# A four-layer graph network: the lists of the matrix build are loaded for two buckets at once, and each range's first product opens its PSUM banks

## The chip, the cores and the metric

The kernel runs on 1 core of one Trainium2 chip, as one program. The metric is the device time in microseconds (us). Its engines are TensorE (PE; its weight loads are listed apart as PEld), VectorE (DVE), ScalarE (ACT), GpSimd (POOL) and SyncE (SP). A q behind an engine's name (DVEq, PEldq) marks an instruction of its sequencer, which computes registers, waits and branches.

## The reference, cut to what matters

Four graph layers with a layernorm after each work on 6250 nodes of 128 features and 100000 edges:

```
edge_index = jnp.stack([src, dst])
x = _layernorm(x + _L0_gnn_ref(x, edge_index, ...))   # two hops over the edges, then two linear layers
x = _layernorm(x + _L1_gnn_ref(x, edge_index, ...))   # hypergraph: nodes = src, hyperedges = dst (2500 of them)
x = _layernorm(x + _L2_gnn_ref(x, edge_weight, ...))  # weighted sum over edges
x = _layernorm(x + _L3_gnn_ref(x, edge_index, ...))   # attention over edges
# the sums over edges that the layers share
agg = segment_sum(norm[:, None] * x[src], dst, num_segments=n)
```

The change is in one preparatory stage that several of these sums use: a matrix `edge_counts` with a row for each node (as source) and a column for each of the first 2560 nodes (as destination), that holds how many edges go from the one to the other.

## The kernel before, in words

Earlier stages sort the edges into 49 buckets by source (`src >> 7`, so 128 nodes a bucket) and write them as tiles of 128 edges, one edge a partition. In `m.meta` each tile has, for each partition, its destination and its source.

`bucket_lists` finds, for each bucket, where three ranges of destinations lie in its tiles. The ranges are `PARTS = ((0, 1), (1, 3), (3, 5))`, in PSUM banks of `KB` = 512 columns: one bank, two banks, two banks. For each bucket and range it stores three integers in the table `m.startI`: the first tile, the number of pairs of tiles, and how many pairs all earlier lists have. So a bucket has 9 integers of 4 bytes, at 36 bytes times its number.

`build_counts` builds the matrix, a bucket at a time, in the phase "build". Four engines run the same walk over the buckets, each in its own program: bucket 0, then a loop of 24 rounds that does an odd bucket and then an even one. Within a bucket all is ordered by semaphores:

- PE and DVE each first load the bucket's 9 integers into registers (`lists`, the load is at L1130). `bounded` (L1135) prepares one of them.
- DVE makes, for each tile, two one-hot matrices in bf16: of the source within the bucket (L1202, 128 by 128) and of the destination within the range (L1204, 128 by 512 or by 1024). There are two buffers, one for each tile of a pair. DVE may fill a buffer once PE has released it (`used`); PE may use it once DVE has announced it (`ready`).
- PE opens the range's banks with a product of zeros (L1170), so that all real products can accumulate, then for each tile multiplies the one-hots into one bank or two (L1177), and at the end closes each bank with a product of one column (L1180), which announces `summed`.
- ACT copies each finished bank to an SBUF row (L1156) and announces `emptied`, for which L1170 waits in the next bucket. SP stores the row of 1.28 MB when five banks are in it (L1141).

The pairs of tiles are a loop with a register as its bound, at L1172 on PE and L1197 on DVE. All engines meet at a barrier before and after the phase, so that its length is that of its slowest chain.

## Time and profile before

| what | value |
|---|---|
| median of 3 runs | 7867.82 us (7810.16 to 7903.07) |
| the profiled execution, its own time | 7873.77 us |
| its span, first to last instruction | 7872.0 us |
| mean granted TensorE clock over the span | 0.76 |
| phase "build", about | 1735 to 2581 us |
| buckets, ranges in the build | 49, 147 |

The span is 1.8 us shorter than the execution's own time. Rows with "idle before" tell how long the engine did nothing ahead of an instruction and what released it; "issue" there means that the profile shows nothing it waited for, which is where its sequencer was still busy with registers, loads or branches. A granted clock of 1.00 is TensorE at 2.4 GHz and 0.50 at 1.2 GHz.

### The profile page before, as it was taken

The numbers are of one execution on the slowest core, as the hardware profiler recorded it, in microseconds if no ns is written. First come the engines' busy times: TensorE is split into PE (matmuls) and PEld (weight loads), VectorE is DVE, ScalarE is ACT, GpSimd is POOL, SyncE is SP. The second block draws the span as 40 slices with busy tenths as digits, with TensorE's granted clock in tenths as the row PEclk, the third lists the DMA queues.
The fourth block names the chain that finished last, engine by engine and source line by source line (L and its number), as shares of the span: only waits on it lengthen the run. The fifth ranks groups of instructions, "written<-read, shape, count | busy, mean of one in ns | idle before, by whom it ended". The sixth has DMA issues, their size and how long they took to land. (4 is left out here: it accounts for less than half of the span.)

```text
span 7872.0 us, 98123 instructions
## 1 busy us (share of the span) xinstructions
PE 3812.2 (48%) x16163; PEld 2422.8 (31%) x16164; DVE 3389.4 (43%) x11703; ACT 1127.3 (14%) x3853; POOL 3603.0 (46%) x3613
## 2 busy tenths in 40 slices
PE   1600150016666775775945554333333356666665
PEld 0300030001111342443423332232322256665663
DVE  4946370026666444114021113333333555665666
ACT  0000000001111000002000001000000244444443
POOL 0045777710000684660056664666666155555550
PEclk9999999987777896887955555555555578888886
DMA  9411111261111563652711111111111233333332
GB/s 129 72 30 36 48 42 53 53 23 78 75 78 73 202 210 106 220 168 87 274 43 45 45 45 42 45 44 43 44 44 44 48 95 95 95 98 95 95 98 35
DMA packets 674873, 648.60 MB, mean 82 GB/s; under 512 B 495848, under 2 KB 564441, under 8 KB 655638
## 3 DMA queue, kind: packets, MB, share of 16 engines
q1 hardware_dynamic: 546182, 379.55, 18.1%
q0 software_dynamic: 128384, 266.34, 12.2%
q14 instruction: 151, 1.24, 0.1%
q10 hardware_dynamic: 144, 1.28, 0.0%
q8 instruction: 12, 0.20, 0.0%
HBM read 502.61 MB, written 144.27 MB: 82 GB/s over the span
## 5 line engine op out<-in xcount | busy, mean ns | idle before, releaser
L828 POOL DMA_INDIRECT bucketed_edges<-edge_rows,idx x784 | 817.6, 1043 | 784.0 <-issue 725.3
L483 POOL DMA_INDIRECT gathered<-node_table,idx x576 | 624.4, 1084 | 1130.7 <-ACT idx L471 958.4
L1337 POOL DMA_INDIRECT gathered<-node_table_xq,idx x832 | 796.3, 957 | 752.8 <-issue 223.7
L359 POOL DMA_INDIRECT gathered<-node_table,idx x816 | 772.7, 947 | 495.9 <-issue 249.8
L374 PE MATMUL ps<-onehots,gathered 128*128 128x128 f32 x1632 | 430.6, 443 | 846.7 <-DVE agg L402 609.0
L663 POOL DMA_INDIRECT gathered<-node_table,idx x588 | 556.1, 946 | 330.7 <-issue 171.7
L430 PE MATMUL ps<-gathered,junk 128*128 128x512 f32 x1182 | 622.4, 636 | 125.7 <-DMA gathered<-edge_counts 125.6
L678 PE MATMUL ps<-onehots,gathered 128*128 128x128 f32 x1176 | 467.7, 501 | 409.3 <-DMA gathered<-node_table,idx 394.9
L374 PEld LDWEIGHTS ps<-onehots,gathered 128*128 128x128 f32 x1632 | 365.1, 327 | 912.2 <-issue 834.3
L1177 PE MATMUL ps<-onehots 128*128 128x512 bf16 x1152 | 472.4, 487 | 187.0 <-DVE onehots L1204 183.9
L678 PEld LDWEIGHTS ps<-onehots,gathered 128*128 128x128 f32 x1176 | 294.6, 311 | 582.4 <-DMA gathered<-node_table,idx 559.4
L389 DVE TENSOR_SCALAR onehots<-iota,off_t,ew_t 128x128 f32<-128x128 f32 x832 | 258.2, 368 | 411.1 <-issue 376.1
L1426 PE MATMUL ps<-Wh,attend_slots 128*128 128x128 f32 x1664 | 405.9, 330 | 59.0 <-issue 56.0
L1427 PE MATMUL ps<-side_rows,attend_slots 128*128 x1664 | 386.7, 319 | 24.6 <-issue 24.6
L863 PE MATMUL ps<-gathered 128*128 128x49 bf16 x784 | 125.1, 222 | 544.6 <-DVE gathered L846 427.4
L499 PEld LDWEIGHTS ps<-onehots,gathered 128*128 128x128 f32 x1152 | 229.4, 217 | 504.4 <-issue 356.0
L402 DVE TENSOR_TENSOR agg<-agg,ps 128x128 f32 x816 | 233.5, 286 | 346.0 <-issue 289.1
L694 DVE TENSOR_TENSOR onehots<-ps,off_members 128x512 f32<-128x512 f32 x150 | 103.2, 689 | 648.0 <-DMA gathered<-node_table,idx 341.2
L534 DVE TENSOR_TENSOR onehots<-ps,off_t 128x512 f32<-128x512 f32 x156 | 107.0, 690 | 608.4 <-remote 237.6
L1202 DVE TENSOR_SCALAR onehots<-iota_b,side_rows,bF 128x128 bf16<-128x128 bf16 x722 | 227.2, 315 | 326.9 <-issue 204.7
L499 PE MATMUL ps<-onehots,gathered 128*128 128x128 f32 x1152 | 257.1, 316 | 208.0 <-DMA gathered<-node_table,idx 92.9
L1426 PEld LDWEIGHTS ps<-Wh,attend_slots 128*128 128x128 f32 x1664 | 311.2, 232 | 87.7 <-issue 85.1
(373 smaller groups left out, 6729.2 us busy)
## 6 DMA issues: line engine op xcount, KB each, us to landing
gathered<-edge_counts SPq DMA_DIRECT2D x99, 1280.0 KB
edge_counts<-gathered SPq DMA_DIRECT2D x49, 1280.0 KB
gathered<-node_table,idx POOLq DMA_INDIRECT x1980
bucketed_edges<-edge_rows SPq DMA_DIRECT2D x52, 544.0 KB, 12.5
edge_rows<-bucketed_edges SPq DMA_DIRECT2D x208, 128.0 KB
gathered<-edge_counts SPq DMA_DIRECT2D x48, 512.0 KB
side_rows<-edge_counts SPq DMA_DIRECT2D x48, 512.0 KB
edge_rows<-in_edge_attr_dram SPq DMA_DIRECT2D x108, 128.0 KB
```

The lines of the kernel that those rows point to most:

```text
L359: nc.gpsimd.indirect_dma_start(g[:, k, :], None, table, bass.IndirectOffsetOnAxis(m.idx[:, k:k + 1], 0)).then_inc(S["landed"][k], 16)
L374: last = nc.tensor.matmul(m.ps[:, q, e * P:(e + 1) * P], g[:, k, :], m.oh[:, k, :], start=True, stop=True)
L430: mm = nc.tensor.matmul(m.ps[:, k, :], m.junk[:, j, :], row_piece(m, j, k), start=first, stop=False)
L483: nc.gpsimd.indirect_dma_start(g[:, k, :], None, a.table, bass.IndirectOffsetOnAxis(m.idx[:, k:k + 1], 0)).then_inc(S["landed"][k], 16)
L499: last = nc.tensor.matmul(sums[q % NS], g[:, k, :], m.oh[:, k, :], start=e == 0, stop=e == G - 1)
L663: nc.gpsimd.indirect_dma_start(g[:, k, :], None, a.table, bass.IndirectOffsetOnAxis(m.idx[:, k:k + 1], 0)).then_inc(S["landed"][k], 16)
L678: last = nc.tensor.matmul(m.ps[:, q, 0:P], g[:, k, :], m.oh[:, k, :], start=e == 0, stop=e == G - 1)
L828: nc.gpsimd.indirect_dma_start(a.bucketed, bass.IndirectOffsetOnAxis(m.idx[:, k:k + 1], 0), m.erow[:, k, :], None).then_inc(S["scattered"] ...
L1177: last = T.matmul(m.ps[:, k, :], ohs[h], ohd[h][:, (k - k0) * KB:(k - k0 + 1) * KB], start=False, stop=False)
L1337: nc.gpsimd.indirect_dma_start(g[:, k, :], None, a.table2, bass.IndirectOffsetOnAxis(m.idx[:, k:k + 1], 0)).then_inc(S["landed"][s], 16)
L1426: T.matmul(out, m.eT[:, 2 * h + e // 2, :], m.Wh[:, e % 2, :], start=True, stop=False)
L1427: last = T.matmul(out, m.ohT[:, G * h + e, :], m.side[:, bass.ds(start[e], P)], start=False, stop=True)
```

## The change

The table of integers is laid out anew, still 9 integers a bucket: first tile and pairs of each range, then the three counts of earlier pairs. The walk over the buckets becomes `walk_lists`: in the loop each of PE and DVE loads the 18 integers of an odd bucket and the even one behind it with one instruction, at the start of the odd bucket. On PE the first pair of tiles of a range is written ahead of the loop, and the product of its first tile overwrites the banks (`start=True`); the product of zeros is gone, and the wait for `emptied` is one for the range instead of one for each bank. For that each list has at least two pairs: the lengths are raised to 3 tiles, which counts as two pairs.

```diff
--- before.py
+++ after.py
@@ -45,6 +45,7 @@
 KW = NK * KB
 PARTS = ((0, 1), (1, 3), (3, 5))
 NR = len(PARTS)
+ROWL = 3 * NR
 WB = KB * max(b - a for a, b in PARTS)
 SPLIT = (E - (P - 1) * NT) // U
 DUMP = BT * P
@@ -1043,8 +1044,7 @@
     inb, rev, fwd, f = (m.gather[0:NB, k * BT:(k + 1) * BT] for k in range(4))
     one, two = m.gather[:, 4 * BT:5 * BT], m.gather[:, 5 * BT:6 * BT]
     first, past = m.lists[PB, 0:NR + 1], m.lists[PB, 6:7 + NR]
-    rowF = m.gather[0:1, 6 * BT:6 * BT + 3 * NB * NR]
-    three = rowF.rearrange("p (b k c) -> p b k c", k=NR, c=3)
+    rows = m.gather[0:1, 6 * BT:6 * BT + ROWL * NB].rearrange("p (b c) -> p b c", c=ROWL)
     pairs, ends = (m.gather[0:1, 7 * BT + j * NB * NR:7 * BT + (j + 1) * NB * NR] for j in range(2))
     halves = lambda t: t.rearrange("p (h t) -> p h t", h=2)
     with phase(nc, "lists", "dve cmp marked counted taken listed rows") as (S, block):
@@ -1075,18 +1075,21 @@
             step(V.tensor_scalar(first, first, -1.0, float(BT), ALU.mult, ALU.add))
             step(V.tensor_scalar(first, first, float(BT - 1), None, ALU.min))
             step(V.tensor_tensor(past, past, first, ALU.subtract))
-            V.tensor_scalar(past, past, 1.0, None, ALU.max).then_inc(S["listed"], 1)
+            step(V.tensor_scalar(past[:, 0:NR], past[:, 0:NR], 3.0, None, ALU.max))
+            V.tensor_scalar(past[:, NR:NR + 1], past[:, NR:NR + 1], 1.0, None, ALU.max).then_inc(S["listed"], 1)
             v.wait_ge(S["rows"], 2 * NR)
+            table = m.startI[0:1, 0:ROWL * NB].rearrange("p (b c) -> p b c", c=ROWL)
+            by_bucket = lambda t: t.rearrange("p (b k) -> p b k", k=NR)
             for q in range(NR):
-                step(V.tensor_copy(three[:, :, q, 0], m.ps[0:1, 5, q * NB:(q + 1) * NB]))
-                step(V.tensor_scalar(three[:, :, q, 1], m.ps[0:1, 5, (NR + q) * NB:(NR + q + 1) * NB], 1.0, None, ALU.add))
-            step(V.tensor_copy(m.startI[0:1, 0:3 * NB * NR], rowF))
-            step(V.tensor_scalar(m.startI[0:1, 0:3 * NB * NR].rearrange("p (i c) -> p i c", c=3)[:, :, 1],
-                                 m.startI[0:1, 0:3 * NB * NR].rearrange("p (i c) -> p i c", c=3)[:, :, 1], 1, None, ALU.arith_shift_right))
-            step(V.tensor_copy(pairs, m.startI[0:1, 0:3 * NB * NR].rearrange("p (i c) -> p i c", c=3)[:, :, 1]))
+                step(V.tensor_copy(rows[:, :, 2 * q], m.ps[0:1, 5, q * NB:(q + 1) * NB]))
+                step(V.tensor_scalar(rows[:, :, 2 * q + 1], m.ps[0:1, 5, (NR + q) * NB:(NR + q + 1) * NB], 1.0, None, ALU.add))
+            step(V.tensor_copy(table[:, :, 0:2 * NR], rows[:, :, 0:2 * NR]))
+            for q in range(NR):
+                step(V.tensor_scalar(table[:, :, 2 * q + 1], table[:, :, 2 * q + 1], 1, None, ALU.arith_shift_right))
+                step(V.tensor_copy(by_bucket(pairs)[:, :, q], table[:, :, 2 * q + 1]))
             step(V.tensor_tensor_scan(ends, m.ones[0:1, 0:1].to_broadcast([1, NB * NR]), pairs, 0.0, ALU.mult, ALU.add))
             step(V.tensor_tensor(ends, ends, pairs, ALU.subtract))
-            step(V.tensor_copy(m.startI[0:1, 0:3 * NB * NR].rearrange("p (i c) -> p i c", c=3)[:, :, 2], ends))
+            step(V.tensor_copy(table[:, :, 2 * NR:], by_bucket(ends)))
 
         @block.tensor
         def _(pe):
@@ -1125,14 +1128,23 @@
                 body(eng.snap(i * 2 + 1), 1, i)
                 body(eng.snap(i * 2 + 2), 0, i + 1)
 
-        def lists(eng, engine, b):
-
-            got = nc.values_load_multi_w_load_instructions(m.startI[0:1, bass.ds(b * (3 * NR), 3 * NR)], engines=[engine])[1]
-            return [got[3 * k:3 * k + 3] for k in range(NR)]
-
-        def bounded(eng, before):
-
-            return eng.snap(nc.s_assert_within(before, 0, NK * (BT + NB)))
+        def walk_lists(eng, engine, body):
+
+            def load(b, n):
+                got = nc.values_load_multi_w_load_instructions(m.startI[0:1, bass.ds(b * ROWL, n * ROWL)], engines=[engine])[1]
+                return [got[ROWL * k:ROWL * (k + 1)] for k in range(n)]
+            body(0, load(0, 1)[0])
+            with eng.Fori(0, (NB - 1) // 2) as i:
+                b = eng.snap(i * 2 + 1)
+                odd, even = load(b, 2)
+                body(b, odd)
+                body(eng.snap(i * 2 + 2), even)
+
+        def parts(eng, row):
+
+            bounded = lambda x: eng.snap(nc.s_assert_within(x, 0, NK * (BT + NB)))
+            for k, (k0, k1) in enumerate(PARTS):
+                yield k0, k1, row[2 * k], row[2 * k + 1], bounded(row[2 * NR + k])
 
         @block.sync
         def _(sp):
@@ -1162,23 +1174,22 @@
             pe.sem_inc(S["used"], 2)
             pe.sem_inc(S["emptied"], NK)
 
-            def body(b, e, u):
-                at = lists(pe, mybir.EngineType.PE, b)
-                for r, (k0, k1) in enumerate(PARTS):
-                    for k in range(k0, k1):
-                        pe.wait_ge(S["emptied"], b * NK + k + 1)
-                        T.matmul(m.ps[:, k, :], m.zerob[:, :], zeros, start=True, stop=False)
-                    n, before = at[r][1], bounded(pe, at[r][2])
-                    with pe.Fori(0, n) as j:
-                        c = pe.snap((before + j) * 2)
+            def body(b, row):
+                for k0, k1, lo, n, before in parts(pe, row):
+                    def pair(c, first):
                         for h in range(2):
                             pe.wait_ge(S["ready"], c + (h + 1))
                             for k in range(k0, k1):
-                                last = T.matmul(m.ps[:, k, :], ohs[h], ohd[h][:, (k - k0) * KB:(k - k0 + 1) * KB], start=False, stop=False)
+                                last = T.matmul(m.ps[:, k, :], ohs[h], ohd[h][:, (k - k0) * KB:(k - k0 + 1) * KB],
+                                                start=first and h == 0, stop=False)
                             last.then_inc(S["used"], 1)
+                    pe.wait_ge(S["emptied"], b * NK + k1)
+                    pair(pe.snap(before * 2), True)
+                    with pe.Fori(1, n) as j:
+                        pair(pe.snap((before + j) * 2), False)
                     for k in range(k0, k1):
                         T.matmul(m.ps[:, k, 0:1], m.zerob[:, :], m.zerob[:, 0:1], start=False, stop=True).then_inc(S["summed"], 1)
-            walk(pe, body)
+            walk_lists(pe, mybir.EngineType.PE, body)
 
         @block.vector
         def _(v):
@@ -1189,14 +1200,12 @@
             v.wait_ge(S["iota"], 1)
             step(V.tensor_copy(iotaK, iotaI))
 
-            def body(b, e, u):
-                at = lists(v, mybir.EngineType.DVE, b)
-                for r, (k0, k1) in enumerate(PARTS):
+            def body(b, row):
+                for k0, k1, lo, n, before in parts(v, row):
                     w = (k1 - k0) * KB
-                    lo, n, before = at[r][0], at[r][1], bounded(v, at[r][2])
                     with v.Fori(0, n) as j:
                         c = v.snap((before + j) * 2)
-                        t = v.snap(nc.s_assert_within(lo + j * 2, 0, BT, skip_runtime_bounds_check_because="a list ends at the last tile"))
+                        t = v.snap(nc.s_assert_within(lo + j * 2, 0, BT + 2, skip_runtime_bounds_check_because="a list ends at the last tile"))
                         for h in range(2):
                             v.wait_ge(S["used"], c + (h + 1))
                             V.tensor_scalar(ohs[h], m.iotab[:, :], m.meta[:, bass.ds(t + h, 1), 2], m.bF[:, bass.ds(b, 1)],
@@ -1204,7 +1213,7 @@
                             V.tensor_scalar(ohd[h][:, 0:w], iotaK[:, 0:w], m.meta[:, bass.ds(t + h, 1), 1], -float(k0 * KB),
                                             ALU.subtract, ALU.is_equal).then_inc(S["ready"], 1)
 
-            walk(v, body)
+            walk_lists(v, mybir.EngineType.DVE, body)
 
 
 def member_lists(nc, m):
```

PE, the loop of the walk, the start of the odd bucket's second range (destinations 512 to 1535, two banks), before. L1169 computes the wait's value, L1135 prepares the count of earlier pairs:

```order
L1180 MATMUL ps<-zero_b 128x1
L1169 ISA
L1170 MATMUL ps<-zero_b 128x512
L1169 ISA
L1170 MATMUL ps<-zero_b 128x512
L1135 ISA x2
L1172 UNCONDITIONAL_BRANCH
L1172 ISA
L1177 MATMUL ps<-onehots 128x512 x2
```

and the same place in the changed kernel:

```order
L1191 MATMUL ps<-zero_b 128x1
L1145 ISA x2
L1186 ISA
L1181 ISA
L1183 MATMUL ps<-onehots 128x512 x2
L1181 ISA
L1183 MATMUL ps<-onehots 128x512 x2
L1188 UNCONDITIONAL_BRANCH
L1188 ISA
L1183 MATMUL ps<-onehots 128x512 x2
```

The two products of zeros are gone, the products of the range's first two tiles stand ahead of the loop's branch, and only one instruction computes a wait on `emptied`.

DVE, the same loop, from the end of the odd bucket's last range to the first one-hot of the even bucket, before:

```order
L1204 TENSOR_SCALAR onehots<-junk,side_rows 128x1024
L1197 REGISTER_ALU
L1197 COMPARE_AND_BRANCH
L1130 ISA
L1130 TENSOR_LOAD start_i
L1135 ISA x2
L1197 UNCONDITIONAL_BRANCH
L1197 ISA
L1202 ISA x2
L1202 TENSOR_SCALAR onehots<-iota_b,side_rows,bF 128x128
```

and in the changed kernel:

```order
L1213 TENSOR_SCALAR onehots<-junk,side_rows 128x1024
L1206 REGISTER_ALU
L1206 COMPARE_AND_BRANCH
L1145 ISA x2
L1206 UNCONDITIONAL_BRANCH
L1206 ISA
L1211 ISA x2
L1211 TENSOR_SCALAR onehots<-iota_b,side_rows,bF 128x128
```

The load between the odd bucket and the even one is gone. The one at the start of the loop's round is still one instruction; it fills 18 registers where it filled 9.

## Rows read from the trace of the kernel before

**Rows 1.** Windows: the matrix build as one stretch (columns as its first line says)
```profile
core 0: us, PE busy (x) PEld busy (x) DVE busy (x) ACT busy (x) POOL busy (x), PEclk, DMA share, GB/s
...
1735.00:2580.00 845.00, 557.25 (x1642) 126.38 (x1642) 515.82 (x1446) 132.91 (x243) 0.67 (x1) 0.75 0.18 74
```

**Rows 2.** Lines by form, 1733 to 2585 us: busy us, mean ns | idle before, releasers
```profile
L1177 PE MATMUL ps<-onehots 128*128 128x512 bf16 x1152 | 472.4, 487 | 187.0 <-DVE onehots L1204 183.9
L1202 DVE TENSOR_SCALAR onehots<-iota_b,side_rows,bF 128x128 bf16<-128x128 bf16 x722 | 227.2, 315 | 326.9 <-issue 204.7 <-PE ps L1177 93.2
L1204 DVE TENSOR_SCALAR onehots<-junk,side_rows 128x1024 bf16<-128x1024 f16 x430 | 209.1, 486 | 0.6
...
L1170 PE MATMUL ps<-zero_b 128*128 128x512 bf16 x245 | 101.4, 488 | 105.7 <-issue 77.3 <-ACT gathered L1156 28.3
```

**Rows 3.** Source view of L1130, the list loads: all 49, then single ones
```profile
L1130 DVEq TENSOR_LOAD <-start_i x49: 862/2075/2099, 1736.5 to 2565.4; - x49
...
L1130 DVEq TENSOR_LOAD <-start_i x1: 864/864/864, 2009.1 to 2009.1; - x1
...
L1130 DVEq TENSOR_LOAD <-start_i x1: 2082/2082/2082, 2025.1 to 2025.1; - x1
...
L1130 PEldq TENSOR_LOAD <-start_i x1: 2427/2427/2427, 2025.7 to 2025.7; - x1
...
L1130 DVEq TENSOR_LOAD <-start_i x1: 2074/2074/2074, 2043.3 to 2043.3; - x1
```

**Rows 4.** Source views of other loads of the table: one value, four, sixteen
```profile
L646 DVEq TENSOR_LOAD <-start_i x50: 298/304/318, 3968.5 to 4808.4; - x50
...
L103 DVEq TENSOR_LOAD <-start_i x208: 340/344/357, 6342.7 to 7741.5; - x104
...
L103 DVEq TENSOR_LOAD <-start_i x8: 1098/1100/1111, 5391.8 to 5555.5; - x8
```

**Rows 5.** Timeline of DVE where a bucket's first range begins (start us, us)
```profile
2010.95 0.32 DVE L1202 TENSOR_SCALAR onehots<-iota_b,side_rows,bF 128x128 bf16<-128x128 bf16 x1 [1.71 <-issue]
...
2013.02 0.32 DVE L1202 TENSOR_SCALAR onehots<-iota_b,side_rows,bF 128x128 bf16<-128x128 bf16 x1 [0.65 <-PE ps L1177]
...
2028.08 0.31 DVE L1202 TENSOR_SCALAR onehots<-iota_b,side_rows,bF 128x128 bf16<-128x128 bf16 x1 [3.18 <-issue]
...
2029.90 0.32 DVE L1202 TENSOR_SCALAR onehots<-iota_b,side_rows,bF 128x128 bf16<-128x128 bf16 x1 [0.41 <-issue]
...
2046.35 0.31 DVE L1202 TENSOR_SCALAR onehots<-iota_b,side_rows,bF 128x128 bf16<-128x128 bf16 x1 [2.90 <-issue]
```

**Rows 6.** Timeline of PE about two range changes of one bucket
```profile
2017.01 1.02 PE L1170 MATMUL ps<-zero_b 128*128 128x512 bf16 x2
2017.94 1.83 PE L1177 MATMUL ps<-onehots 128*128 128x512 bf16 x4
...
2021.52 0.59 PE L1170 MATMUL ps<-zero_b 128*128 128x512 bf16 x2
2022.29 0.60 PE L1177 MATMUL ps<-onehots 128*128 128x512 bf16 x2 [0.18 <-DVE onehots L1204]
```

**Rows 7.** Timeline of DVE in the two-bank ranges of that bucket
```profile
2017.15 0.31 DVE L1202 TENSOR_SCALAR onehots<-iota_b,side_rows,bF 128x128 bf16<-128x128 bf16 x1 [0.67 <-PE ps L1177]
...
2019.36 0.32 DVE L1202 TENSOR_SCALAR onehots<-iota_b,side_rows,bF 128x128 bf16<-128x128 bf16 x1 [0.67 <-PE ps L1177]
...
2021.50 0.32 DVE L1202 TENSOR_SCALAR onehots<-iota_b,side_rows,bF 128x128 bf16<-128x128 bf16 x1 [0.54 <-issue]
...
2023.31 0.32 DVE L1202 TENSOR_SCALAR onehots<-iota_b,side_rows,bF 128x128 bf16<-128x128 bf16 x1 [0.27 <-issue]
```

**Rows 8.** Windows of that bucket, split where the granted clock changes
```profile
2012.80:2019.60 6.80, 4.91 (x12) 1.02 (x11) 4.31 (x13) 0.59 (x1) 0.00 (x0) 0.50 0.35 145
2019.60:2029.80 10.20, 5.33 (x22) 1.41 (x21) 5.62 (x16) 2.15 (x4) 0.00 (x0) 1.00 0.21 89
```

**Rows 9.** Groups by line, 1728 to 1735 us, the end of the list stage
```profile
L1084 DVE TENSOR_SCALAR start_i<-start_i 1x147 int32<-1x147 int32 x1 | 0.3, 252 | 0.0
```

## The prediction

> **What bounds the kernel now.** The change touches the end of the list stage and the phase "build"; nothing else. I read the windows first, to size the phase: 845 us of the span, with neither PE (557 us) nor DVE (516 us) busy all the time, the clock 0.75 on average and the DMA engines at 18% [rows 1]. So two engines take turns there, and the next view is the groups by line and form. DVE makes 722 pairs of one-hots, its idle time of 327 us stands before L1202 and most of it is "issue", that is, its own sequencer [rows 2]. PE's 245 products of zeros are 101 us busy [rows 2]. The reader is to ask of each whether it lies on the chain DVE to PE to DVE that paces the phase. The source view of L1130 and the timeline show where a bucket begins: DVE stands for 1.71, 3.18 or 2.90 us [rows 5] while the sequencer loads nine integers in 0.86, 2.08 or 2.07 us [rows 3]. Both engines load at about the same time, and neither has work for the other.
>
> **The load, which is the largest term.** The three single loads are of buckets 16, 17 and 18. The same instruction serves 16 and 18, so it is the address that makes 0.86 or 2.07 us. Through all 49 loads on DVE the pattern holds: the 13 buckets with a number divisible by four take 0.86 to 0.87 us (the very first 1.10), the other 36 take 2.07 to 2.10. A bucket's list starts at 36 bytes times its number, which is a multiple of 16 just for those 13. Other loads of the same table agree: one value 0.304 us, four values from a multiple of 16 bytes 0.344, sixteen 1.100 [rows 4]. From an aligned start the cost goes by groups of four: 0.344 + 3 x 0.25 = 1.10 for sixteen, and 0.344 + 2 x 0.26 = 0.86 for nine. From any other start it goes by single values: 0.304 + 8 x 0.2214 = 2.075 for nine.
>
> The new double load always starts at an odd bucket, never at a multiple of 16 bytes, and has 18 values: 0.304 + 17 x 0.2214 = 4.07 us against 2.08, so +1.99 us. Odd buckets in the loop are 24: **+47.8 us**. Bounds: if 18 values from there went by fours after all, five groups cost 0.344 + 4 x 0.25 = 1.34, -0.74 each or -18 us; above, PE's dearest load was 2.43 us [rows 3], by which 18 cost 0.304 + 17 x 0.266 = 4.82, with PE some 0.15 us late once DVE's two buffers are full, +4 us more. I take the price by single values, because nine odd-started values have it in 24 of 24 loads.
>
> The Trainium skill, "Runtime: NRT & Kernel Launch", section "Instruction fetch mechanics", puts such a load at about 200 ns a register even in bulk. This trace has 230 for nine unaligned values, and 96 and 69 for nine and sixteen aligned ones. By the page's rule 24 loads of 18 values cost what 48 of nine do, the two loads together would be near zero in place of +5.7, and the total +21.
>
> **The load that goes.** Even buckets in the loop are 24; 12 of them (16 and the like) begin with 1.71 us of idle DVE, 12 (18 and the like) with 2.90 [rows 5]. What is late next is what every change of range costs with no load: 0.54 at the high clock, where the last range ends, and 0.67 at the low one [rows 7]. At 0.55: 12 x (1.71 - 0.55) + 12 x (2.90 - 0.55) = **-42.1 us**. The two loads together: **+5.7 us**. ACT, which copies the banks out, and the stores behind it hold slack: 133 us of 845 busy and 18% of the DMA engines [rows 1], so nobody there waits for the shorter change of bucket.
>
> **The products of zeros.** They are 101 us of PE and I take them at nothing, by the timeline of PE. At the change from one bank to two, at the low clock, two of them run from 2017.01 to 2018.03 in the records, and the first real product starts at 2017.94 [rows 6], right behind the one-hot that DVE began at 2017.15 (0.31 + 0.49 us of work) [rows 7]. At the next change they run from 2021.52 and end at 2022.11, and PE waits 0.18 us more for DVE [rows 6]. At a bucket's start PE opens its bank while DVE makes its first one-hot. Bounds: 0, and -0.1 us for each of 98 inner changes, -10 us. The closing products of one column stay. Moving two first products ahead of PE's loop leaves their number: 1152. Had any list only one pair, the floor of two would add work; the one-hots, counted list by list in the timeline, give 2 or 3 pairs in all 147 lists (the third range has 2 in each of 49), so it adds none.
>
> **The clock.** The build swings between the two levels in every bucket. In the bucket of the rows TensorE is at 0.50 (1.2 GHz) from 2012.8 to 2019.6 and at 1.00 (2.4 GHz) to 2029.8 [rows 8]. It rose while six 512-column products stood nearly end to end (two of zeros, four real, 2017.01 to 2019.77) and fell after the load's gap and the thin one-bank work. The level is worth time only in the two-bank ranges: a pair of tiles takes 2019.36 - 2017.15 = 2.21 us at the low one, where DVE waits for PE, and 2023.31 - 2021.50 = 1.81 at the high one, where DVE paces [rows 7], 0.40 a pair. Without the products of zeros TensorE has a gap of 0.8 us just ahead of that rise. I expect it later in some buckets: if half of them do the two pairs of the last range at the low level, 49 x 0.5 x 2 x 0.40 = **+20 us**. Bounds: 0, and, if the clock stays low through all five banks' work, some 2.3 pairs a bucket, 49 x 2.3 x 0.40 = +45 us.
>
> **The rest.** The list stage gets one more step of the kind of L1084 and four more short ones, 0.25 us each [rows 9]: +1.2 us. The code also shifts, and that has a price which no row assigns beforehand: a pair in the one-bank range takes 2013.02 - 2010.95 = 2.07 us in the even bucket's copy of the loop and 1.82 in the odd one's [rows 5], with the same instructions. There are 48 such pitches in each copy, so +12 or -12 us; I take 0.
>
> **The sum.** 5.7 + 0 + 20 + 1.2 = +27 us on the profiled execution's 7873.8 us, 7901. That execution lies 6 us above the median of the runs, so I predict 7867.8 + 27 = 7895 us. The phase would grow from 846 to about 873 us.
>
> **The rivals.** (a) *The wide load is cheap.* If 18 values go by fours, the loads give -18 - 42 = -60 us, with the clock's +20 and the list stage -39: 7829. For it: aligned loads do so. Against it: 36 of 36 unaligned ones did not. (b) *The products of zeros held the clock up.* This is the slower side. Their place is the start of the two-bank ranges. If without them the clock rises in no bucket before the load's gap, the sum is 5.7 + 45 + 1.2 = +52, with the code's shift up to +64: 7920 to 7932. All other terms together are between +7 and, with the inner changes' whole 10 us gained, -3; so it decides the sign once about one bucket in ten keeps the low clock (0.1 x 45 = 4.5 us). It can't reach 1% by itself, which would be 79 us. For it: the rise follows dense work of which a third were zeros. Against it: the real products alone are still four in each 2.21 us. [...] (c) *The clock does not care.* The zeros were fewer than a fifth of PE's columns (245 of 1397 products), the rises stay where they are, and the sum is +7, or -3 with the inner changes: 7865 to 7875.
>
> **How the numbers follow.** Chances: forecast 0.45, (a) 0.12, (b) 0.18, (c) 0.25. A measurement of this kernel tells about 1% from no change: its three runs span 93 us, 1.2%. Even (a) is -0.5% and (b) +0.8%, so the chance that it is the same within 1% is 0.91; 0.04 for faster, if the loads and the layout both go well and the runs scatter low, and 0.05 for slower. The range must hold (a) nearly whole and (b) with its scatter: 7829 at the low end, 7932 at the high end, and some 10 us of scatter of a median of runs: 7825 to 7942.
>
> **What would show it.** The source view of the list load should have 24 loads of about 4.1 us and one of 1.1 on DVE; DVE's idle at an odd bucket's start about 5.1 us, and at an even one's 0.5 to 0.7. L1170 gone, 1152 products left. The mean clock of the build below 0.75, and more two-bank pairs at 2.21. I am wrong if the load of 18 takes under 3 us, or if two-bank pairs keep their 1.81 in the last range of nearly all buckets; and wrong in kind if a stage other than the build moves by more than 20 us.

## The result, and the profile after

The changed kernel takes 7921.56 us, the median of 15 runs (7895.68 to 7982.26), against 7856.02 for the kernel before in 15 runs of the same series. The ratio is 1.0089, with a 95% interval of 1.0067 to 1.0111: slower by 0.9%, some 70 us. The forecast was +27 us and 7895, with a range of 7825 to 7942. The time lies in the range, but the step is two and a half times as large as forecast.

The profiled execution took 7982.26 us (span 7980.5), the longest of the 15. Its first one-hot of the build starts at 1781.6 us, that of the kernel before at 1738.5: 43 us came in ahead of the build, where the program is the same but for 1 us of list steps. Over the profiled kernels of this study, which ahead of that point differ only in a few short steps (one with a phase of loads ahead of it is left out), the first one-hot lies between 1732 and 1806 us. So whole times of single executions are not compared below; the stretch from the first one-hot of the build to the last is. The windows view of that stretch, changed kernel (columns as in [rows 1]):

```profile
1781.60:2688.90 907.30, 517.53 (x1394) 112.61 (x1395) 514.50 (x1444) 132.83 (x243) 0.00 (x0) 0.67 0.17 69
```

The same stretch of the kernel before, a few us shorter than that of [rows 1]:

```profile
1738.40:2579.40 841.00, 556.07 (x1638) 125.99 (x1639) 514.41 (x1444) 132.91 (x243) 0.00 (x0) 0.75 0.18 75
```

It grew by 66 us at an unchanged busy time of DVE (514.5 and 514.4 us). The groups by line of the changed kernel, for [rows 2]:

```profile
L1183 PE MATMUL ps<-onehots 128*128 128x512 bf16 x1152 | 515.2, 531 | 398.9 <-DVE onehots L1213 385.6 <-ACT gathered L1168 12.5
L1211 DVE TENSOR_SCALAR onehots<-iota_b,side_rows,bF 128x128 bf16<-128x128 bf16 x722 | 227.2, 315 | 393.4 <-issue 254.4 <-PE ps L1183 109.3
```

DVE's idle time ahead of its one-hots is 393 us in place of 327, most of the growth under "issue"; each real product is 531 ns in the mean in place of 487, because more of them run at the low clock (the windows say 0.67 in place of 0.75). The products of zeros are gone. The source view of the list load, for [rows 3]:

```profile
L1134 PEldq TENSOR_LOAD <-start_i x25: 1048/6390/6457, 1778.2 to 2653.6; - x25
L1134 DVEq TENSOR_LOAD <-start_i x25: 1104/6269/6286, 1779.7 to 2653.0; - x25
```

Here is the term that was mis-sized: the 24 loads of 18 values take 6.13 to 6.29 us on DVE, where 4.07 was forecast. The timeline of DVE where a bucket begins, for [rows 5], first an odd bucket and then the even one behind it:

```profile
2060.30 0.32 DVE L1211 TENSOR_SCALAR onehots<-iota_b,side_rows,bF 128x128 bf16<-128x128 bf16 x1 [7.23 <-issue]
...
2076.75 0.31 DVE L1211 TENSOR_SCALAR onehots<-iota_b,side_rows,bF 128x128 bf16<-128x128 bf16 x1 [0.65 <-issue]
```

7.23 us idle in place of 3.18, and 0.65 in place of 1.71 or 2.90. And the two-bank pairs, for [rows 7], in the last range of the bucket before that:

```profile
2049.03 0.31 DVE L1211 TENSOR_SCALAR onehots<-iota_b,side_rows,bF 128x128 bf16<-128x128 bf16 x1 [0.54 <-PE ps L1183]
...
2051.24 0.32 DVE L1211 TENSOR_SCALAR onehots<-iota_b,side_rows,bF 128x128 bf16<-128x128 bf16 x1 [0.46 <-PE ps L1183]
```

That pair took 2.21 us in a range where it had taken 1.81. The stretch by its parts, from the starts of the one-hots and the idle times in the timeline:

| part | before, us | after, us | difference x count | us |
|---|---|---|---|---|
| DVE idle at the start of an odd bucket, mean | 3.17 | 7.34 | +4.17 x 24 | +100.2 |
| at the start of an even bucket, mean | 2.32 | 0.66 | -1.66 x 24 | -39.7 |
| one-bank pair in the even bucket, start to start | 2.06 | 1.81 | -0.25 x 47 | -11.6 |
| change from one bank to two, last start to first start | 2.07 | 2.08 | 0.00 x 49 | +0.1 |
| two-bank pairs: 13 us between their starts, 4 in the last one of each bucket | | | | +17.3 |
| sum | 841.0 | 907.3 | | +66.3 |

In the last range, the pair that can be timed (49 of them, one a bucket) took the high clock's 1.66 to 1.81 us in 42 buckets before and in 20 after. The change from one bank to two, where the products of zeros used to stand, takes as long without them.

### The profile page after: what moved, and what is told of

It is laid out like the page before. It is cut to its first block and busy times, and to the rows that moved or that the text cites. A ratio compares the mean times of both kernels' runs of the same rounds, so it can differ in the third digit from the quotient of the medians.

```text
span 7980.5 us, 97152 instructions
## 1 busy us (share of the span) xinstructions
PE 3777.5 (47%) x15918; PEld 2414.8 (30%) x15919; DVE 3393.4 (43%) x11708; ACT 1127.0 (14%) x3853; POOL 3576.9 (45%) x3613
## 5 line engine op out<-in xcount | busy, mean ns | idle before, releaser
L829 POOL DMA_INDIRECT bucketed_edges<-edge_rows,idx x784 | 798.2, 1018 | 845.5 <-issue 760.2
L375 PE MATMUL ps<-onehots,gathered 128*128 128x128 f32 x1632 | 430.6, 443 | 854.6 <-DVE agg L403 608.2
L1183 PE MATMUL ps<-onehots 128*128 128x512 bf16 x1152 | 515.2, 531 | 398.9 <-DVE onehots L1213 385.6
L679 PE MATMUL ps<-onehots,gathered 128*128 128x128 f32 x1176 | 467.7, 501 | 409.4 <-DMA gathered<-node_table,idx 398.1
L500 PE MATMUL ps<-onehots,gathered 128*128 128x128 f32 x1152 | 258.6, 317 | 206.4 <-DMA gathered<-node_table,idx 90.1
L1447 PE MATMUL ps<-onehots,gathered 128*128 128x128 f32 x1664 | 275.7, 316 | 128.7 <-DVE onehots L1482 88.4
```

The source lines that it names most:

```text
L375: last = nc.tensor.matmul(m.ps[:, q, e * P:(e + 1) * P], g[:, k, :], m.oh[:, k, :], start=True, stop=True)
L500: last = nc.tensor.matmul(sums[q % NS], g[:, k, :], m.oh[:, k, :], start=e == 0, stop=e == G - 1)
L679: last = nc.tensor.matmul(m.ps[:, q, 0:P], g[:, k, :], m.oh[:, k, :], start=e == 0, stop=e == G - 1)
L829: nc.gpsimd.indirect_dma_start(a.bucketed, bass.IndirectOffsetOnAxis(m.idx[:, k:k + 1], 0), m.erow[:, k, :], None).then_inc(S["scattered"] ...
L1183: last = T.matmul(m.ps[:, k, :], ohs[h], ohd[h][:, (k - k0) * KB:(k - k0 + 1) * KB], start=first and h == 0, stop=False)
```

## The experiments

The 18-value load was first measured by itself.

**Loads alone.** The kernel before, with a phase ahead of the build in which only DVE loads (the values are used as indices of a small copy, whose output nobody reads):

```diff
+            with v.Fori(0, 8) as i:
+                use(nc.values_load_multi_w_load_instructions(m.startI[0:1, bass.ds(i + 448, 1)], engines=[mybir.EngineType.DVE], ...)[1])
...
+                use(nc.values_load_multi_w_load_instructions(m.startI[0:1, bass.ds(i + 448, 20)], engines=[mybir.EngineType.DVE], ...)[1])
```

> The kernel before, with an extra phase of loads alone ahead of the build: VectorE loads 1, 2, 4, 5, 8, 9, 10, 12, 13, 16, 17, 18 and 20 values from each of 8 start places in a row (0 to 28 bytes past a multiple of 64), nothing else running. The phase computes nothing that is used. Theory A (the price is in the instruction: number of values and start place): 18 values from an unaligned start take 6.27 us here too, although PE is silent, and the steps show where the price leaves 0.22 us a value. Theory B (two engines in each other's way: PE and DVE load at once in the build): 18 values alone take 0.304 + 17 x 0.22 = 4.07 us, 20 take 4.5. Both: from multiples of 16 bytes the price goes by fours, 9 values 0.86, 16 values 1.10.

Source views of five of the lines, for 4, 9, 16, 18 and 20 values; each line ran from eight start places, two of which are multiples of 16 bytes. The three numbers are minimum, median and maximum in ns:

```profile
L1127 DVEq TENSOR_LOAD <-start_i x8: 352/958/965, 1759.2 to 2232.5; - x8
...
L1130 DVEq TENSOR_LOAD <-start_i x8: 849/2064/2067, 1765.8 to 2241.5; - x8
...
L1134 DVEq TENSOR_LOAD <-start_i x8: 1105/3603/3608, 1782.4 to 2264.3; - x8
...
L1136 DVEq TENSOR_LOAD <-start_i x8: 1579/4044/4049, 1794.5 to 2281.3; - x8
...
L1137 DVEq TENSOR_LOAD <-start_i x8: 1362/4484/4490, 1801.1 to 2290.3; - x8
```

The minimum is that of the two aligned starts, median and maximum those of the other six. From an unaligned start the price is 0.22 us a value up to twenty; 18 take 4.04 us, as the prediction had it. From an aligned start it goes by fours at 0.25 us each, and each value left over costs about as much as a group of four (18 values 1.58 us, 20 values 1.36). So theory A fell: the price of 6.27 us is not in the instruction. Something in the build adds 2.2 us.

**The double load undone.** The changed kernel, with one line for each bucket:

```diff
-                odd, even = load(b, 2)
-                body(b, odd)
-                body(eng.snap(i * 2 + 2), even)
+                body(b, load(b, 1)[0])
+                c = eng.snap(i * 2 + 2)
+                body(c, load(c, 1)[0])
```

> The changed kernel, but each bucket loads its own 9 values at its start, as before; the overwriting first product stays. From the first one-hot to the last the build took 840.9 us before and 907.2 after. Theory 'the wide load does the harm': 907.2 - 24 x (7.33 + 0.66) + 24 x 3.17 + 12 x 1.71 + 12 x 2.92 = 847 us, ratio to before about 1.001. Rival 'the overwriting product or the peeled pair does the harm': the build stays over 880 us and the ratio over 1.005.

```profile
1737.50:2587.10 849.60, 534.45 (x1394) 114.31 (x1394) 514.07 (x1444) 132.85 (x243) 0.00 (x0) 0.66 0.18 74
```

The ratio to before is 0.9979 (0.9950 to 1.0007), so the loss in the whole time is gone. Of the 66 us in the build 58 are, and those were the double load's. The build is still 9 us longer than the 841 of the kernel before, though it no longer has the dear one-bank pair (-12): the two-bank pairs cost 20 us more, at a clock of 0.66 in this row.

**The zeros put back.** The changed kernel with the product of zeros in place of the overwriting first one:

```diff
-                                                start=first and h == 0, stop=False)
+                                                start=False, stop=False)
...
-                    pe.wait_ge(S["emptied"], b * NK + k1)
-                    pair(pe.snap(before * 2), True)
-                    with pe.Fori(1, n) as j:
+                    for k in range(k0, k1):
+                        pe.wait_ge(S["emptied"], b * NK + k + 1)
+                        T.matmul(m.ps[:, k, :], m.zerob[:, :], zeros, start=True, stop=False)
+                    with pe.Fori(0, n) as j:
```

> The changed kernel, but with the products of zeros back (and no peeled pair on PE); the double load stays. Theory 'the clock was lost with the zeros': about 18 us come back against the changed kernel, the build takes 889 us, pairs in the third range are at 1.81 us again in at least 40 of 49 buckets, ratio to before 1.006. Rival 'the long gap behind the 18-value load lets the clock fall': the pairs at 2.21 us stay and the build takes 905 to 910 us.

```profile
1732.10:2628.10 896.00, 550.62 (x1638) 139.96 (x1638) 513.95 (x1444) 132.87 (x243) 0.00 (x0) 0.75 0.17 70
```

The ratio to before is 1.0077 (1.0043 to 1.0112). The clock is back at 0.75 with the long loads still there, and the pair in the last range is at 1.66 to 1.81 us in 44 of 49 buckets: the long gap is not what kept the clock low. The edit also puts the peeled pair back into its loop, and no run has the one without the other. But the peeled pair moved none of the real work: the change from one bank to two takes 2.07 or 2.08 us, and the pair behind it at the low clock 2.21, in the kernel before and in the changed one alike. What is left as the difference on PE is the zeros.

Only 11 us came back in place of 18. In this kernel the first two-bank pair at the low clock takes up to 2.36 us, in the kernel before 2.21. The timeline of PE and DVE at such a place:

```profile
2028.63 0.21 PE L1192 MATMUL ps<-zero_b 128*128 128x1 bf16 x1
2028.85 0.32 DVE L1212 TENSOR_SCALAR onehots<-iota_b,side_rows,bF 128x128 bf16<-128x128 bf16 x1 [0.68 <-PE ps L1183]
...
2028.93 1.03 PE L1188 MATMUL ps<-zero_b 128*128 128x512 bf16 x2
...
2029.76 1.91 PE L1183 MATMUL ps<-onehots 128*128 128x512 bf16 x4
```

The products of zeros start 0.30 us behind the closing product, in the kernel before 0.08 (2017.01 behind 2016.93), and the first real product starts 0.91 us behind the start of DVE's one-hot, there 0.79 [rows 6, rows 7]. The likely reason is the order of the program: the changed code prepares the count of earlier pairs ahead of the products of zeros, the kernel before behind them; no run moved that alone. In 45 of 49 buckets the first two-bank pair takes 2.31 us or more here, 5.5 us together by the sum of these pairs (113.8 against 108.3), so without this some 17 us would have come back. All versions below that keep the zeros have this order.

**What lies under the load.** With DVE alone the load takes 4.04 us, in the build 6.27. Two things are beside it there: PE's own load, and the store of the finished bucket, 1.31 MB (128 rows of 2560 numbers of 4 bytes). Windows of 1 us of the changed kernel about the load of 2053.3 to 2059.5 us on DVE; the last two columns are the DMA engines' share and GB/s:

```profile
2054.00:2055.00 1.00, 0.05 (x3) 0.00 (x0) 0.00 (x0) 0.91 (x2) 0.00 (x0) 1.00 0.00 0
2055.00:2056.00 1.00, 0.00 (x0) 0.00 (x0) 0.00 (x0) 0.17 (x1) 0.00 (x0) 1.00 0.00 0
2056.00:2057.00 1.00, 0.00 (x0) 0.00 (x0) 0.00 (x0) 0.00 (x0) 0.00 (x0) 1.00 0.78 328
2057.00:2058.00 1.00, 0.00 (x0) 0.00 (x0) 0.00 (x0) 0.00 (x0) 0.00 (x0) 0.58 1.20 492
2058.00:2059.00 1.00, 0.00 (x0) 0.00 (x0) 0.00 (x0) 0.00 (x0) 0.00 (x0) 0.50 0.90 379
2059.00:2060.00 1.00, 0.00 (x0) 0.00 (x0) 0.00 (x0) 0.00 (x0) 0.00 (x0) 0.50 0.27 113
```

The store's packets move in the windows from 2056 to 2060, in the load's second half. In the kernel before the nine-value load of 2025.1 us ends at 2027.2, and the packets start within the same microsecond:

```profile
2026.00:2027.00 1.00, 0.00 (x0) 0.00 (x0) 0.00 (x0) 0.71 (x2) 0.00 (x0) 1.00 0.00 0
2027.00:2028.00 1.00, 0.00 (x0) 0.00 (x0) 0.00 (x0) 0.00 (x0) 0.00 (x0) 1.00 0.39 164
2028.00:2029.00 1.00, 0.52 (x2) 0.19 (x2) 0.79 (x3) 0.00 (x0) 0.00 (x0) 1.00 1.03 430
```

Two runs tell the neighbours apart. In the first, SP issues the store one bank later:

```diff
-                hold(sp, S["emptied"], b * NK + 2 * NK)
+                hold(sp, S["emptied"], b * NK + 2 * NK + 1)
...
             walk(act, body)
+            act.wait_ge(S["emptied"], NB * NK + NK)
+            act.sem_inc(S["emptied"], 1)
```

> The changed kernel, but the store of a bucket's row of 1.28 MB is issued only when the next bucket's first bank is copied out, some 6 us later, so that it no longer runs under the 18-value load. Theory C (register loads get dearer while the store's packets move): the loads take 4.05 us as when loaded alone, DVE idles 5.1 us at an odd bucket in place of 7.3, the build takes 907 - 24 x 2.2 = 854 us. Theory B (PE and DVE slow each other's loads): the loads stay at 6.27 us and the build at 907.

```profile
L1134 DVEq TENSOR_LOAD <-start_i x25: 1103/4060/4081, 1797.4 to 2623.1; - x25
```

The stretch in the windows view:

```profile
1799.30:2656.90 857.60, 512.85 (x1369) 113.16 (x1395) 514.40 (x1444) 132.90 (x243) 0.00 (x0) 0.67 0.18 73
```

The load falls to 4.06 us, and the build by 50 us to 857.6. PE's load lies beside DVE's all the while here, and 4.06 is within 0.02 us of what DVE needs alone. PE's own loads of 18 values fall as well, from 6.39 to 4.27 us:

```profile
L1134 PEldq TENSOR_LOAD <-start_i x25: 1049/4269/4302, 1795.9 to 2623.6; - x25
```

In the second, PE loads nine values for each bucket and only DVE loads 18:

```diff
-                odd, even = load(b, 2)
+                odd, even = load(b, 2) if wide else (load(b, 1)[0], None)
...
-                body(eng.snap(i * 2 + 2), even)
+                body(c, even or load(c, 1)[0])
...
-            walk_lists(pe, mybir.EngineType.PE, body)
+            walk_lists(pe, mybir.EngineType.PE, body, False)
```

> The changed kernel, but PE loads 9 values for each bucket, and only DVE loads 18. Theory B (PE and DVE slow each other's loads): DVE's load has PE's beside it for 2 us instead of 6, and falls to 4.5 us or less. Theory C (the store's packets do it): DVE's 18 values stay at 6.2 to 6.3 us, and PE's 9 at 2.1 to 2.4.

```profile
L1134 PEldq TENSOR_LOAD <-start_i x49: 847/2192/2429, 1788.7 to 2711.3; - x49
L1134 DVEq TENSOR_LOAD <-start_i x25: 1108/6249/6276, 1790.1 to 2687.6; - x25
```

DVE's load stays at 6.25 us with PE's load beside it for a third of the time. The build of this version takes 931.9 us, 25 more than that of the changed kernel. At an even bucket PE still loads while DVE has its values already, and DVE then waits for PE in the one-bank range: pairs there take up to 3.55 us, and 22 of the 25 us are in them.

So theory B fell and theory C holds. While the store's 1.31 MB leave, at 328 to 492 GB/s in the full windows, the register load gets on at about a third of its pace (an estimate: 2.2 us are lost in some 3.4). Both halves of the 100 us at odd buckets are now measured: 24 x 2.0 for the nine values more, 24 x 2.2 for the store.

The kernel before has the same effect in small, in PE's loads of nine values. PE starts its load 0.6 us behind DVE. In the odd bucket below, its load lasts until 2028.1 and the packets start in the microsecond from 2027; in the even bucket behind it no packet moves before the load ends at 2046.1:

```profile
L1130 PEldq TENSOR_LOAD <-start_i x1: 2427/2427/2427, 2025.7 to 2025.7; - x1
...
L1130 PEldq TENSOR_LOAD <-start_i x1: 2167/2167/2167, 2043.9 to 2043.9; - x1
```

It is so in all 36 unaligned loads: the 23 during which bytes of the store moved took 2.39 to 2.43 us, the 13 others 2.17 to 2.20.

**The lists aligned.** Each bucket's nine integers at 48 bytes times its number. Three kernels, with the single load or the double one, and with or without the zeros:

```diff
-ROWL = 3 * NR
+ROWL = 12
...
-            step(V.tensor_copy(table[:, :, 2 * NR:], by_bucket(ends)))
+            step(V.tensor_copy(table[:, :, 2 * NR:3 * NR], by_bucket(ends)))
...
-                got = nc.values_load_multi_w_load_instructions(m.startI[0:1, bass.ds(b * ROWL, n * ROWL)], engines=[engine])[1]
+                got = nc.values_load_multi_w_load_instructions(m.startI[0:1, bass.ds(b * ROWL, n * ROWL - ROWL + 3 * NR)], engines=[engine])[1]
```

Single loads, first product overwriting (the list load's source view and the stretch):

> The changed kernel with each bucket's list at 48 bytes times its number (a row of 12 integers, 3 unused) and each bucket loading its own 9 values. Theory 'the start place sets the price': all 49 loads take 0.86 us, so the build takes 847 - 36 x 1.21 = 803 us, ratio to before about 0.995. Rival 'not the start place but the bucket': 36 loads stay at 2.08 us and the build at 847 us.

```profile
L1134 DVEq TENSOR_LOAD <-start_i x49: 854/859/1107, 1730.3 to 2523.5; - x49
```

```profile
1732.20:2537.40 805.20, 521.70 (x1394) 113.05 (x1395) 514.05 (x1444) 132.84 (x243) 0.00 (x0) 0.69 0.19 78
```

The ratio is 0.9933 (0.9899 to 0.9968). All 49 loads but the first take 0.85 to 0.89 us. With the zeros put back in that kernel:

> Lists at 48 bytes times the bucket's number, each bucket loads its own 9 values, and the products of zeros are back: the kernel before with an aligned table. Theory 'the zeros keep the clock up in the last range': against the same kernel without them (build 805 us) some 11 to 18 us less, so 787 to 794 us, and the last range's pairs at 1.8 us in at least 40 of 49 buckets. Rival 'the overwriting product is better once the loads are short': over 805 us. Ratio to before about 0.992.

```profile
1796.60:2587.10 790.50, 550.46 (x1613) 139.80 (x1637) 514.36 (x1444) 132.84 (x243) 0.00 (x0) 0.77 0.19 80
```

The ratio is 0.9941 (0.9920 to 0.9962), from another series than the one above, and the intervals overlap, so the whole times do not tell the two apart. The stretch of the build does: 790.5 in place of 805.2 us, with the clock at 0.77 in place of 0.69. The double load, aligned, first product overwriting (the unused integers are set to zero as well):

> The changed kernel with lists at 48 bytes times the bucket's number, and the double load kept: 21 values from a multiple of 16 bytes. Theory 'price by fours from an aligned start' (16 values 1.10, 20 values 1.36, 9 values 0.85 us when loaded alone): 21 take 1.6 us, the build takes 805 - 24 x (1.70 - 0.66) + 24 x (1.6 - 0.86) = 798 us, ratio to before about 0.993. Rival 'a double load is bad however it starts': the build stays over 830 us.

```profile
L1135 DVEq TENSOR_LOAD <-start_i x25: 1102/1612/1637, 1784.2 to 2556.7; - x25
```

```profile
1786.10:2588.30 802.20, 518.96 (x1369) 114.06 (x1394) 514.50 (x1444) 132.88 (x243) 0.00 (x0) 0.68 0.19 78
```

The ratio is 0.9948 (0.9930 to 0.9965): a double load is no harm where it takes 1.61 us (1.36 for twenty values and 0.25 for one more) and ends before the store's packets start: none moved during any of the 25. By the stretch it is 3 us shorter than with two single loads, in one profiled execution of each, which the ratios do not confirm.

**All that helped, together.** Aligned lists, the double load, and the zeros kept (the edits above, combined):

> Lists at 48 bytes times the bucket's number, the double load (21 values, aligned), and the products of zeros kept: of all versions the one that keeps what helped. From the measured parts: the aligned single-load version with zeros took 790.4 us in the build; the double load moved the version without zeros by 802.1 - 805.1 = -3 us; so 787 us, ratio to before 0.992 to 0.994. Rival: in the low-clock pairs PE's code costs 2.3 in place of 2.2 us as in the other versions with zeros, and the double load gains nothing, 790 to 795 us.

```profile
1791.70:2576.80 785.10, 541.14 (x1613) 140.04 (x1637) 514.61 (x1444) 132.87 (x243) 0.00 (x0) 0.79 0.19 80
```

785 us, 56 less than before, and a ratio of 0.9922 (0.9907 to 0.9937): faster by 0.8% than the kernel before, where the changed kernel is slower by 0.9%.

**The code's place.** The kernel before, with three or six more steps ahead of the loop, which only repeat the step that fills `bF`:

```diff
             step(V.tensor_copy(iotaK, iotaI))
+            for _ in range(3):
+                step(V.tensor_scalar(m.bF[:, :], m.iota[:, 0:NB], -float(P), None, ALU.mult))
```

> The kernel before with three more short, idle steps on DVE ahead of the build's loop, so that the same loop code lies some instructions further on; nothing else changes. Theory 'the place of the code sets the branch's price': the one-bank range's pair in the even bucket (2.06 us in the kernel before, 1.81 in every other version) falls to 1.81 us, or another loop becomes dear. Rival 'it belongs to the order of the instructions in that loop': it stays 2.06 us and all other pitches stay.

> As the run with three more steps, with six. Theory 'place of the code': one of the six loops of the walk, or none, is dear by 0.25 us a pair, and which one it is depends on the number of steps. Rival: the even bucket's one-bank range stays at 2.06 us in both.

Timeline of DVE at an even bucket's start with three more steps, for [rows 5], and the windows of the two:

```profile
2075.42 0.32 DVE L1204 TENSOR_SCALAR onehots<-iota_b,side_rows,bF 128x128 bf16<-128x128 bf16 x1 [1.70 <-issue]
...
2077.25 0.32 DVE L1204 TENSOR_SCALAR onehots<-iota_b,side_rows,bF 128x128 bf16<-128x128 bf16 x1 [0.42 <-issue]
```

```profile
1805.90:2635.70 829.80, 559.23 (x1613) 126.40 (x1637) 514.52 (x1444) 132.83 (x243) 0.00 (x0) 0.75 0.18 76
```

```profile
1787.90:2617.80 829.90, 553.52 (x1614) 125.98 (x1638) 514.48 (x1444) 132.84 (x243) 0.00 (x0) 0.76 0.18 76
```

The pair takes 2077.25 - 2075.42 = 1.83 us in place of 2.07, and the build 829.8 and 829.9 us in place of 841.0, for nothing but the place of the loop. With six more steps it is the same. In neither did another loop become dear, but in the run with loads alone one did. Its build is that of the kernel before, further on by the phase ahead of it. DVE's timeline there at an odd bucket's start and then at an even one's:

```profile
2559.87 0.31 DVE L1232 TENSOR_SCALAR onehots<-iota_b,side_rows,bF 128x128 bf16<-128x128 bf16 x1 [3.32 <-issue]
...
2561.93 0.31 DVE L1232 TENSOR_SCALAR onehots<-iota_b,side_rows,bF 128x128 bf16<-128x128 bf16 x1 [0.65 <-PE ps L1207]
...
2577.18 0.31 DVE L1232 TENSOR_SCALAR onehots<-iota_b,side_rows,bF 128x128 bf16<-128x128 bf16 x1 [1.59 <-PE ps L1207]
...
2579.01 0.31 DVE L1232 TENSOR_SCALAR onehots<-iota_b,side_rows,bF 128x128 bf16<-128x128 bf16 x1 [0.41 <-issue]
```

Here the odd bucket's pair takes 2.06 us (2.04 to 2.12 in all 48) and the even one's 1.83 (mean 1.81), the reverse of the kernel before. So both halves of the theory hold: the place sets the price, and the dear loop wanders. What makes a place bad was not tried.

## Why the prediction was right, and where it was not

**The load of 18 values: the step that was mis-sized.** "0.304 + 17 x 0.2214 = 4.07 us against 2.08, so +1.99 us" is right for the load alone (4.04) and with the store delayed (4.06). It was 6.27 in the kernel, because a load that is 2 us longer reaches into the store that starts behind it. The term was +47.8 us and came out at +100, outside the bounds that the prediction gave it: by its upper price of 4.82 us a load it would have been +66 and 4 more for PE. The prediction looked at PE as the neighbour of that load, and at ACT and the stores only for who would wait; it did not ask what the longer load would run into. The windows of 1 us of the kernel before, which show the packets starting in the microsecond in which the load ends, were at hand. So was the sign itself: the prediction read PE's dearest load, 2.43 us, as a price of 0.266 us a value, but it was a load of 2.17 that the store had reached.

**The load that goes.** Forecast -42.1 us, measured -40: 0.66 us stays where 0.55 was taken. The price by start place that was read from the 49 loads held in every kernel, and with 12 integers a bucket it gave a gain of its own, 805 against 850 us.

**The products of zeros** were taken at nothing on the chain, and in the kernel before they are at nothing: the change from one bank to two takes 2.07 us with them and 2.08 without, and the pair behind it 2.21 us at the low clock in both. They did come onto the chain, by 0.1 us, in the versions that open the banks a little later.

**The clock.** Forecast +20 us, and the mechanism was right. Against the kernel before, moved by three steps so that all its loops are cheap (829.8 us), the version without zeros and with the same single loads takes 849.6: +20 us. With aligned loads it is +15 (805.2 against 790.5), with aligned double loads +17 (802.2 against 785.1), with unaligned double loads +11 (907.3 against 896.0); those three are net of the 0.1 us above. Each stretch is from one profiled execution. But the mean clock over the whole span, which every run has, splits in the same way: 0.748 to 0.754 in the 15 runs of the changed kernel, 0.757 to 0.766 in the 10 with the zeros put back, and 0.753 to 0.756 against 0.766 to 0.768 with aligned double loads.

"Half of them" was near: 29 of 49 buckets no longer have the last range's timed pair at its high-clock time, 7 before. Rival (b) was this at full price, and did not happen: TensorE reached the high clock in the two-bank ranges of all 49 buckets before and of 39 after. The Trainium skill, "TensorE: Matmul & The Clock Gate", section "HAM oscillation — how this bites in real kernels", describes short bursts of matmuls with waits between them, each of which starts at half clock. The trace agrees in part: in the bucket of [rows 8] the clock falls to 0.50 at 2012.8 us, but 1.9 us after the bucket's first one-hot (2010.95), and is back at 1.00 at 2019.6. These runs add that products of no use to the result can be what brings the clock up.

**The rest.** The list stage went from 56.1 to 57.2 us, +1.1 where +1.2 was forecast. The code's place was given as +12 or -12 and taken at 0; it was -12.

**The sum.** 100.2 - 39.7 + 17.3 - 11.6 + 1.1 = +67 us, against +70 (53 to 87) by the ratio. That 7921.56 lies in the range is luck: the room above the forecast was made for rival (b), whose 7920 to 7932 it would match, and it was filled by the load, which none of the rivals named. Rival (a), a wide load that goes by fours, is what an aligned table would have made of it, not this one. Rival (c), that the clock does not care, fell. Of the signs named, "24 loads of about 4.1 us" and "5.1 us idle" were wrong, the rest came true. "A stage other than the build moves by more than 20 us" was a bad sign to name: the stretch ahead of the build differs by up to 74 us between profiled executions, although its program is nearly the same in all of them.

## What to carry to other kernels

Before a step on an engine's sequencer is made longer, look in windows of 1 us at what starts just behind it; here 2 us more of register loads cost 4. Lay out tables that are loaded into registers so that every load starts at a multiple of 16 bytes: it was worth 36 x 1.2 us here and costs three unused integers a bucket. And a product that does nothing for the result may still hold TensorE's clock up where DVE and PE take turns, so price its removal by the pairs at either clock, not by its busy time.

## What the runs showed of the hardware

- On DVE alone a load of n registers from SBUF costs 0.31 us for the first and 0.22 for each further value from a start that is no multiple of 16 bytes. From a start that is one it costs 0.35 us for four and 0.25 for each further group of four, and each value left over 0.24 to 0.25. 20 values: 4.48 against 1.36 us. The Trainium skill, "Runtime: NRT & Kernel Launch", section "Instruction fetch mechanics", has about 200 ns a register, also in bulk, for register loads that the page describes as coming from HBM. For these from SBUF the trace is near it from unaligned starts, and from aligned ones the measurement decides, 68 ns a value at 20.
- A register load on PE beside it does not slow DVE's (4.06 us with PE's beside it throughout, 4.04 alone), but a DMA that reads 1.31 MB out of SBUF does: 18 values 6.27 us with it, 4.06 without. PE's load goes from 4.27 to 6.39 us.
- The same loop cost 2.06 or 1.81 us a pair by its place in the program alone, and another loop was the dear one when the code lay elsewhere.
- The kernel before took 7971 and 7977 us (medians of 13 and 11 runs) beside two of the series of experiments, and 7856 and 7875 (15 and 25 runs) in the others: more between series than any version here gained, so only ratios within a series are compared. The series of 7875, 7971 and 7977 ran on three different chips. In the profiles from the first of them the build's first one-hot starts at 1732 to 1738 us, in those from the two others at 1786 to 1806, so half of the difference or more is there ahead of the build; the reason is open. Stretches of the build are compared across these chips above; where the loads are the same, DVE's mean idle at the odd buckets' starts agrees between chips to 0.02 us (3.17 and 3.17, 7.35 and 7.33, 1.97 and 1.97, 2.72 and 2.72).
